# A pre-norm decoder layer on one core: how four input tiles are transposed

## The reference

```python
x = x + _L0_attn_ref(_layernorm(x, axis=-1), L0_attn_Wq, L0_attn_Wk, L0_attn_Wv, L0_attn_Wo)
x = x + _L0_xattn_ref(_layernorm(x, axis=-1), ctx_4096, ...)
x = x + _L0_ffn_ref(_layernorm(x, axis=-1), L0_ffn_weight, L0_ffn_bias)

# _L0_attn_ref
q = (x @ Wq).reshape(b, t, N_HEADS, HEAD_DIM).transpose(0, 2, 1, 3)
k = (x @ Wk).reshape(b, t, N_KV, HEAD_DIM).transpose(0, 2, 1, 3)
v = (x @ Wv).reshape(b, t, N_KV, HEAD_DIM).transpose(0, 2, 1, 3)
q = _apply_rope(q, cos, sin)
k = _apply_rope(k, cos, sin)
scores = jnp.einsum('bhqd,bhkd->bhqk', q, k_h) / math.sqrt(HEAD_DIM)
```

## Time and profile before

| | us |
|---|---|
| median of 3 runs | 480.43 |
| lowest, highest | 476.97, 481.77 |
| the profiled execution | 480.98 |
| its span | 479.1 |

### The profile page before, as it was taken

The page is one execution under the profiler, slowest core; times in us unless marked ns, Lnnn a source line. Parts: engine busy times, 40 slices in busy tenths (PEclk is TensorE's granted clock), DMA queues, the critical chain, the costliest instruction groups (busy, mean ns, idle before and its releaser), DMA issues.

```text
span 479.1 us, 9721 instructions
## 1 busy us (share of the span) xinstructions
PE 441.4 (92%) x3730; PEld 243.4 (51%) x3730; DVE 377.3 (79%) x961; ACT 300.1 (63%) x302; POOL 288.1 (60%) x157
## 2 busy tenths in 40 slices
PE   0899997998999999999999999998998999899896
PEld 0676453554555555555555555555543444446442
DVE  4989873888788888888978899896297568799775
ACT  3586252123787777787778898889745313797633
POOL 5002463143989999999998888888730980707000
PEclk9999998999899999999999999999999999999999
DMA  8563386612041111101153113333087010000044
GB/s 328 179 248 126 115 269 207 212 45 78 28 152 46 47 57 57 55 27 46 48 174 118 45 75 111 114 112 108 25 284 266 23 45 23 1 1 2 2 177 179
DMA packets 21042, 50.93 MB, mean 106 GB/s; under 512 B 4736, under 2 KB 10112, under 8 KB 19712
## 3 DMA queue, kind: packets, MB, share of 16 engines
q1 hardware_dynamic: 19696, 41.79, 25.5%
q10 hardware_dynamic: 1296, 8.45, 5.0%
HBM read 40.67 MB, written 9.44 MB: 105 GB/s over the span
## 4 chain that ended last, share of the span: by engine, by line
PE 54%; DVE 14%; ACT 11%; POOL 11%; issue 5%; DMA 4%; SPq 0%; ACTq 0%; DVEq 0%; POOLq 0%
PE ps L1465 11%; PE ps L1288 9%; PE ps L1371 7%; PE ps L1616 5%; ACT s1reg L566 5%; PE ps L1352 5%; POOL more L1205 4%; PE ps L1333 4%; PE ps L1313 4%; DVE stat L769 3%; POOL s1reg L1205 2%; PE ps L1571 2%; DMA qstack<-in_x 2%; PE ps L1354 2%; DMA rope_scratch<-s1reg 2%
## 5 line engine op out<-in xcount | busy, mean ns | idle before, releaser
L829 DVE CUSTOM_DVE_ANT_0 ps<-ps,causal 128x512 f32<-128x512 f32 (+3 forms) x256 | 120.9, 510 | 19.7 <-PE ps L1333 16.6
L566 ACT ACTIVATE s1reg<-ps 128x1280 f32<-128x1280 f32 x64 | 78.9, 1233 | 44.4 <-PE ps L1354 44.1
L1288 PE MATMUL ps<-xT,wqx 128*128 128x512 f16 x384 | 96.3, 383 | 0.0
L1465 PE MATMUL ps<-wo_reg,xT 128*128 128x512 f16 x384 | 93.0, 379 | 0.0
L1333 PE MATMUL ps<-kreg,qstack 96*128 96x512 f16 (+3 forms) x256 | 61.4, 305 | 5.3 <-DMA qstack<-rope_scratch 3.3
L1352 PE MATMUL ps<-qstack,kreg 98*128 98x512 f16 (+3 forms) x256 | 57.9, 303 | 0.0
L1288 PEld LDWEIGHTS ps<-xT,wqx 128*128 128x128 f16 x384 | 37.2, 98 | 37.3 <-issue 2.1
L1465 PEld LDWEIGHTS ps<-wo_reg,xT 128*128 128x128 f16 x384 | 36.5, 97 | 36.6 <-issue 0.2
L1186 POOL TENSOR_TENSOR s1reg<-s1reg 128x512 f32<-128x512 f32 x11 | 15.9, 1449 | 64.0 <-DVE s1reg L818 63.9
L1205 POOL TENSOR_TENSOR s1reg<-s1reg 128x1280 f16<-128x1280 f32 x19 | 49.8, 2623 | 5.9 <-ACT s1reg L572 5.7
L1205 POOL TENSOR_TENSOR wkv<-s1reg,wkv 128x1280 f16<-128x1280 f32 x18 | 47.2, 2624 | 5.5 <-ACT wkv L572 5.5
(11 more groups left out here) (134 smaller groups left out, 929.4 us busy)
## 6 DMA issues: line engine op xcount, KB each, us to landing
s1reg<-in_weights ACTq DMA_DIRECT2D x8, 1024.0 KB, 5.2
s1reg<-in_ctx SPq DMA_DIRECT2D x16, 512.0 KB, 4.2
qstack<-rope_scratch SPq DMA_DIRECT2D x48, 128.0 KB, 2.6
rope_scratch<-s1reg SPq DMA_DIRECT2D x40, 128.0 KB, 2.2
qstack<-in_x SPq DMA_DIRECT2D x8, 512.0 KB, 5.1
s1reg<-in_x SPq DMA_DIRECT2D x16, 256.0 KB, 3.2
out<-s1reg SPq DMA_DIRECT2D x7, 512.0 KB, 2.7
s1reg<-in_L_ffn_weight SPq DMA_DIRECT2D x5, 512.0 KB, 6.1
```

The lines of the kernel that those rows point to most:

```text
L566: nc.scalar.activation(ebuf[:, j % 2, :], st_ps[:, 0:SCORES], ACT.Exp, scale=EXP_SCALE, bias=P_LOG_SCALE).then_inc(e_done, 1)
L829: last = nc.vector.tensor_tensor_reduce(part, part, causal[:, T - w:T], 1.0, LOWEST, ALU.add, ALU.max, mt[:, G % 2, h, qt:qt + 1])
L1288: last = mm(out_ap, w(ws, k), xT[:, xs, KT * b + k, :], start=(k == 0 and n == 0), stop=(k == KT - 1 and n == 2))
L1465: last = mm(ps[:, bank, :], xT[:, os, KT * b + k, t], wo_sb[:, ws, 4 * h:4 * h + 4, k, :], start=(k == 0 and n == 0), stop=(k == KT - 1 an ...
```

## The change

Tiles 4 to 7 are no longer transposed by TensorE. ScalarE takes the high part of a normalised tile straight from `xin` (`x_high`, one instruction of 1024 columns) and GpSimd the low part (subtract, 1024 columns), both into `xsplit`, three slots in the tensor `more`. SyncE then transposes each part by one DMA from `xsplit` into `xT`, 256 KB each, eight DMAs in all; a tile's two DMAs raise `xt_in[i]` by 16 each. Tile 7 uses the slot of tile 4 again, and so its two parts wait for `xt_in[0]` to be 32. TensorE's `k_tile(2)`, `k_tile(3)` and `v_tile(4)` and later wait for all four `xt_in` (`input_b1`); `xt_lo` now counts batch 0 alone.

```diff
+        xsplit = more[:, 0:6 * D].rearrange("p (t s n) -> p t s n", t=3, s=2)
+        x_hi, x_lo = sem("x_hi"), sem("x_lo")
+        xt_in = [sem(f"xt_in{i}") for i in range(TT)]
...
             next_x(7)
+            for i in range(TT):
+                for hl, made in enumerate((x_hi, x_lo)):
+                    sp.wait_ge(made, i + 1)
+                    sp.dma_start_transpose(xT[:, hl, KT:2 * KT, P * i:P * i + P], xsplit[:, i % 3, hl, :]).then_inc(xt_in[i], 16)
             to_scratch(0)
...
+            def x_high(t):
+                i = t - TT
+                act.wait_ge(xn_ready, t + 1)
+                if i >= 3:
+                    act.wait_ge(xt_in[i - 3], 32)
+                nc.scalar.activation(xsplit[:, i % 3, 0, :], xin[:, i, :], ACT.Copy).then_inc(x_hi, 1)
...
             normalise(5)
-            xt_high(4, 0)
+            x_high(4)
             v_high(1)
             v_high(2)
-            xt_high(4, 1)
             next_weight(1)
             weight_high(2)
             rstd(3)
-            xt_high(5, 0)
-            xt_high(5, 1)
+            x_high(5)
             normalise(6)
             normalise(7)
-            xt_high(6, 0)
+            x_high(6)
             weight_high(3)
-            xt_high(6, 1)
             v_high(3)
             next_weight(2)
-            xt_high(7, 0)
-            xt_high(7, 1)
+            x_high(7)
...
             variance(3)
-            xt_low(4, 0)
             inverse(3, X_SCALE)
-            xt_low(4, 1)
-            xt_low(5, 0)
-            xt_low(5, 1)
             weight_low(2)
             dve.wait_ge(const_in, 48)
             rotate_b(0)
-            xt_low(6, 0)
-            xt_low(6, 1)
-            xt_low(7, 0)
-            xt_low(7, 1)
             scalars()
             rotate_b(1)
...
+            for i in range(TT):
+                pool.wait_ge(x_hi, i + 1)
+                if i >= 3:
+                    pool.wait_ge(xt_in[i - 3], 32)
+                nc.gpsimd.tensor_tensor(xsplit[:, i % 3, 1, :], xin[:, i, :], xsplit[:, i % 3, 0, :], ALU.subtract).then_inc(x_lo, 1)
+
             for n in range(11):
                 rotated_b(n)
...
+            def input_b1():
+
+                for i in range(TT):
+                    pe.wait_ge(xt_in[i], 32)
+
             def k_tile(n):
                 pe.wait_ge(w_lo, 2)
-                pe.wait_ge(xt_lo, NT if n < 2 else 2 * NT)
+                pe.wait_ge(xt_lo, NT)
+                if n >= 2:
+                    input_b1()
...
             v_tile(2)
-            xt(4, 0)
-            xt(4, 1)
-            xt(5, 0)
-            xt(5, 1)
             k_tile(0)
             v_tile(3)
-            xt(6, 0)
-            xt(6, 1)
-            xt(7, 0)
-            xt(7, 1)
             k_tile(1)
             k_tile(2)
```

More of the change, by code:

```diff
@@ L1307, in v_tile @@
                 pe.wait_ge(w_lo, 1)
-                pe.wait_ge(xt_lo, 2 * t + 2 if t < TT else 2 * NT)
+                pe.wait_ge(xt_lo, min(2 * t + 2, NT))
+                if t >= TT:
+                    input_b1()
                 if t >= 2:
@@ L1417, in _ @@
             pe.wait_ge(const_in, 48)
-            pe.wait_ge(xt_lo, 2 * NT)
             pe.wait_ge(v_lo, TT)
```

## The result

The changed kernel takes 484.94 us (median of 8 runs, 484.33 to 486.49). The kernel before took 480.11 us in the runs beside it (476.97 to 481.96, 8 runs). Medians take in every run; ratios leave out the few that were over 1.5% slower than the fastest of their kernel. The ratio is 1.0106, with a 95% interval of 1.0074 to 1.0138: 1.06% slower, 4.8 us. The forecast was 482.7 us. The profiled execution took 485.4 us, with a span of 483.6 us against 479.1 before.

A forecast was written before the change was run, and what follows sets the result against it. Bound: when the first scores start (80.80 us), awaiting rotation, scratch write and query-stack read. Terms +3.15 +1.9 −0.85 +0.7 −2.4 −0.8 = +1.7 us: 482.7 us against 480.98; range 480 to 493.

The forecast's parts named there:

- data: TensorE's k_tile(2) waits for the last transpose, landing at 49.3, and so starts 3.15 us later than before.
- clock on 48 matmuls: After idling before k_tile(2), TensorE runs at the 1.2 GHz level for a while: +1.9 us.
- slack of q tile 4: q tile 4 ended at 61.7 but was rotated at 62.53, so 0.85 us of lateness is absorbed.
- lock of VectorE and GpSimd: At q tile 4's rotation, weight_low(5) begins before GpSimd's sum: +2.05 there, less 1.26 at the low part; net +0.7 us.
- write and read of the stack: Before the first scores, the 8.07 us scratch write gives back half its excess over the 3.4 us median: −2.4 us.
- clock given back at the scores: TensorE's pause before the first scores shrinks from 3.34 to 0.8 us, sparing half of 1.6 us slow clock: −0.8 us.
- the landing of the last transpose: Last transpose of batch 1, after x_low(7): taken as 3.4 us, the median in traffic, landing at 49.3.
- The end of x_low(7): GpSimd's last low part: x_high(7) done at 43.7, the subtract taking about 2.1 us, so ending at 45.9.
- Rival 1: The eight transposes queue behind each other at 3.4 us each, the last landing at 58.5: 492.7 us; chance 22%.
- if SyncE is held by them: A condition under which the prediction fails: the transposes hold SyncE; no size given.
- Rival 2: Before the scores, the write gives nothing back and the clock falls again: +4.9 to +6, 486.5 us; chance 15%.
- within 2 or 3 us of 80.8: A sign that would show the forecast: the first L1341 scores start that near their former time.

The follow-up runs named there:

- Kernel 7: kernel 4 plus 21 matmuls whose result nobody reads, filling TensorE's wait before k_tile(2): 479.61 us, ratio 0.9985.
- kernel 4: The changed kernel with weight chunk 4 requested by SyncE after the last transpose has landed: 481.67 us, ratio 1.0061.
- kernel 2: The changed kernel without the eight transposing DMAs, nothing cleared; batch 1's keys and values projected from batch 0's columns: 480.86 us, ratio 1.0013.
- kernel 9: The changed kernel with two query tiles ahead of batch 1's keys, weight chunk 8 requested earlier and weight_low(6) moved ahead: 476.94 us, ratio 0.9943.
- kernel 11: As kernel 9, with the first sum of the second key tile's rotation ahead of the last low part on GpSimd: 475.91 us, ratio 0.9890.
- kernel 3: The changed kernel with ScalarE requesting weight chunk 4 two steps later, after x_high(7) and rope_high(0): 485.61 us, ratio 1.0117.
- kernel 5: The changed kernel with plain DMA copies of the same 256 KB in place of the transposing DMAs: 482.99 us, ratio 1.0096.
- kernel 6: The changed kernel plus 36 matmuls whose result nobody reads, before TensorE's wait of k_tile(2): 483.9 us, ratio 1.0097.
- kernel 1: The changed kernel without the transposing DMAs, GpSimd clearing batch 1's part of xT at the start instead: 487.03 us, ratio 1.0166.

## Why the prediction was right, and where its sizes were off

The forecast (482.7) lies 0.5% under the result, and the result in the range (480 to 493). But the change itself was forecast at +1.7 us and measured at +4.8: that the time came so near owes much to how small the change is against 480 us. The ratio of 1.0106 sits just over the 1% that I had set between the same (55%) and slower (42%). The mechanism was the one forecast: k_tile(2) waits for the last transpose, the clock falls in that wait, and the write and the pause ahead of the scores give a part back. Term by term, from the two profiled executions (the spans differ by 4.5 us, so 0.4 is left over):

| term | predicted | measured |
|---|---|---|
| data: start of k_tile(2) | +3.15 | +5.94 (52.09 − 46.15) |
| clock on 48 matmuls | +1.9 | +2.4 (12.92 − 10.52) |
| slack of q tile 4 | −0.85 | −0.6 (its rotation 70.23 − 62.53 = +7.70, less the two above) |
| lock of VectorE and GpSimd | +0.7 (2.05 − 1.26 is 0.79) | +0.8 (low part ready at 77.68 instead of 69.21) |
| write and read of the stack | −2.4, of the write alone | −3.0 (8.62 from low part to scores; 11.59 before): write −3.9, read +0.9 |
| clock given back at the scores | −0.8 | −1.4 |
| sum | +1.7 | +4.1 |

**The step that was mis-sized** is the landing of the last transpose: "I take 3.4 us, the median in traffic", so that it "lands at 49.3". The end of x_low(7), 45.9, was right to 0.25 us (45.65). The transpose did take 3.13 us from issue to landing. What the sum left out is that it could not be issued at 45.9: SyncE's queue was held 1.31 us by each of the transposes ahead of it and 4.07 by one, and the last went out at 48.68. I had priced a transfer as issue to landing and given its issue no time. Kernel 7 shows the size: with the load away and the low part as late as here (45.69), the last is issued at 46.0 and lands at 49.3, to the tenth what I had, and the term is +3.35 (49.50 − 46.15) against my +3.15. The 2.6 us that are missing are all beside the load.

**Rival 1**, that the transposes queue behind each other, was half true, for a reason I had named only in the last line ("if SyncE is held by them"). By themselves, 1.31 us apiece, they nearly keep up: I had counted one piece for each 2.1 us, but a tile brings two, 2.6 us of the queue, while the last two low parts come 3 us apart. In kernels 4 and 7 the last was issued 1.0 and 0.3 us after its low part. Beside a 1 MB load they don't keep up. That "the last two run beside the 1 MB weight chunk" stood in my text as a remark; it was worth 2.6 us of start.

**Rival 2** had 486.5 and lies nearer to the result than my sum, but not by what it said: the write gave 3.9 us back, and the slow clock did not come again at the scores. Of my signs, the first scores "within 2 or 3 us of 80.8" failed (5.5 us later), and "if SyncE is held by them" was the case.

**The slow clock in my rows.** I called the 4.84 us of 24 matmuls at 18.01 the 1.2 GHz level. At 81 to 83 us, behind the pause ahead of the scores, the trace of the kernel before grants 0.50; from 18 to 21 us it shows 1.00 beside those slow matmuls, so that row does not bear the level out. In the kernel after, the same 24 took 2.78 us behind the same pause of 1.56 us.

**The estimate of 1.0 us** of transfer from the Trainium skill's "DMA: Bandwidth & Descriptors" ("Latency and other measured facts", 261 GB/s) was near: kernel 4's windows show 192 to 208 GB/s, 1.3 us for 256 KB. The serial reading of the Trainium skill's "VectorE: DVE Perf Modes" ("The three transpose paths", 1309 ns a block) is not borne out here: eight blocks landed in 3.1 us.

**What the transposes on TensorE were worth.** "None of this by itself moves the first scores" held in its number: with no transfer at all (kernel 2) the scores start at 80.78 against 80.80. It is a balance, though, of time saved on TensorE and VectorE and of VectorE held up beside GpSimd, which I had not priced. I had also written that the cover for rotated_b(0) behind the low parts was VectorE's idle time, with rotate_b(1) at 47.3. It came at 48.69, since the ten small instructions took 5.4 us beside GpSimd, against 2.3 before. In this order that was hidden by TensorE's longer wait; in the order of kernels 9 and 11 TensorE waited 2 us for it.

**Unforeseen, without a price:** k_tile(0) now waits 1.38 us for weight_low(1), since TensorE arrives there at 28.93 instead of 31.42, 1.75 us of that by the transposes. TensorE's saved 3.5 us became waiting there and at k_tile(2).

## What to carry to other kernels

Before moving work off a busy engine, look at which wait stands last behind it, and at whom the moved work will hold up. TensorE was 78% busy up to the first scores, yet giving it 3.5 us back brought nothing, because a rotation through three other engines and two transfers set that time. Another order of the same tiles did bring 0.7%. Price a DMA three times: what its issue holds the queue, what it takes of the sixteen engines together with every load in flight, and its landing. And the waits of 4 to 9.5 us on TensorE cost 1.7 to 2.8 us more in clock behind them (48 matmuls in 12.25 to 13.28 us instead of 10.52, kernels after and 3 to 6), so one that can't be covered is worth filling, as long as the filler reaches to its end: in kernel 7 a wait of 1.42 us was left and the clock held, in kernel 6's profiled execution 4.20 us were left and it fell. Last, look in two traces at the same load before an edit is given credit for a start: one load that landed 1.5 us earlier in some executions made up 1.1 of the 3.7 us by which kernel 4 started earlier.

## What the runs showed of the hardware that I had not expected

- A transposing DMA of 256 KB (128 by 1024 in f16) holds SyncE's queue for 1.31 to 1.35 us (kernels after and 4), a copy of the same bytes for 0.65 in the median of kernel 5; beside a 1 MB load single transposes hold it for 4.07 to 5.58 us. Transposes alone keep the DMA engines at a share of 1.0 and move 192 to 208 GB/s (kernel 4, 41 to 47 us).
- With no load in flight one lands in 3.1 to 3.6 us; beside a 1 MB load in 6 to 10 (6.1 to 9.8 in the kernel after), even when the load is requested 0.85 us after it (8.2 us).
- VectorE's instructions of 0.17 us on two columns took up to 2.00 us while GpSimd subtracted 1024 columns. VectorE's timeline of the kernel after, where the one at 43.47 has its usual length, and a weight split that took 4.23 us instead of 2.29, also beside a low part, stands ahead of them:

```profile
37.00 4.23 DVE L811 SCALAR_TENSOR_TENSOR wqx<-s1reg,wqx 128x2048 f16<-128x2048 f32 x1
...
43.47 0.17 DVE L767 TENSOR_SCALAR qs<-qs 128x2 f32<-128x2 f32 x1
43.67 2.00 DVE L768 TENSOR_SCALAR qs<-qs 128x2 f32<-128x2 f32 x1
45.70 1.18 DVE L769 TENSOR_TENSOR qs<-qs 128x2 f32<-128x2 f32 x1
```

- A clear of 128 partitions by 8192 columns on GpSimd at the program's start, in kernel 1, moved TensorE's first key tile back by 5.6 us, though nothing there reads what it writes. A VectorE instruction on two columns, 0.17 us in the kernel after, began 0.45 us behind the clear and ended with it. Kernel 1, GpSimd and VectorE:

```profile
7.71 6.93 POOL L1178 MEMSET xT<- 128x8192 f16 x1
...
8.16 6.50 DVE L780 TENSOR_SCALAR rt<-mv 128x2 f32<-128x2 f32 x1
```
